# A mixture-of-experts layer and a GRU in one kernel: recurrent weights turned by VectorE in 32x32 squares, expert work one scan step later, three steps' rows sent from SBUF to SBUF

## The chip, the cores and the metric

One core of one Trainium2 chip. The metric is the device time of one execution of the program in microseconds (us), the median of several runs.

## What is computed

The input x is 8 sequences of 512 tokens with 256 features. A layer with one shared expert and 8 routed ones (two chosen per token) is added to x; then a GRU runs over the 512 tokens of each sequence, one after the other, and its output is added.

```python
# L0: x = x + (shared + routed) / 3
shared = silu(xf @ w1) * (xf @ w3) @ w2                 # 256 -> 512 -> 256
s = sigmoid(concat([xf, tf]) @ router_W)                # 8 scores, top 2 chosen
h = gelu(einsum('nc,ech->enh', xf, W1e)); y = einsum('enh,ehc->enc', h, W2e)
routed = einsum('ne,enc->nc', combine, y)
# L1: x = x + Ys, H has shape (8, 256)
Xz, Xr, Xh = X @ Wxz.T + bxz, X @ Wxr.T + bxr, X @ Wxh.T + bxh
for t in range(512):
    Z = sigmoid(Xz[t] + H @ Whz.T + bhz);  R = sigmoid(Xr[t] + H @ Whr.T + bhr)
    Ht = tanh(Xh[t] + (R * H) @ Whh.T + bhh)
    H = Z * H + (1 - Z) * Ht;  Y[t] = H @ Whq.T + bhq
```

## The kernel before, in words

**Tiles.** The tokens are cut into 32 tiles of 16 time steps: 8 sequences times 16 steps are 128 rows. Two tiles are a pair. For a pair the up products of the experts (`up`, L1111) run on both tiles at once, in three products of fp32r parts; the down products (`down`, through `product` L1083 in the scan and `full_product` L1119 ahead of it) run tile by tile. `accumulate` (L852) adds an expert's output to x on VectorE.

**Scan.** `body(n)` runs the 16 scan steps of tile n. A step is a ring of short operations on three engines: TensorE's product for gate r (L1247), ScalarE's tanh `t_r` (L693), VectorE's transposes `t_rT` (L982) and the product `rhT` (L985), TensorE's product for the candidate, ScalarE's `t_h` (L713), VectorE's transposes `terms` (L1006) and the scan instruction `hist` (L1009), which gives the next H. All else fills the gaps: each engine's program is written out by hand, and `place_of(n, s)` maps a scan step to a pair p and a place r of 32 in that pair's program; tables by r (`PROJ1`, `UP_ACT2`, `ADD2`, `TANH1`, `LATE_XT2`) say what is done there. `FIRST_STEP` sets the distance between s and r. Three things go by the step s itself and not by r: the ring, the seeds of the gate banks, and `keep_states` (L631), in which ScalarE copies the last tile's 16 states at s = 0.

```python
sp = s + TS * ((n + 1) % 2)
return (n + 1) // 2 + (sp >= FIRST_STEP), (sp - FIRST_STEP) % SPAN
```

**Gate inputs.** `project` multiplies a tile's x by the three input weights `wxT`; `add_bias` (L863) puts the result, half by half (q = 0, 1), into `xproj`. SP stores it to DRAM (`store_inputs`, L474), and `gate_rows` (L480) loads it again in the layout of the scan, `xs`: steps 0 to 7 first, steps 8 to 15 later. ScalarE's `seed_r` (L616) and `seed_zc` (L624) copy a step's row from `xs` to the gate banks. `load_late` (L464, L466) brings the x of later tiles in 17 transfers each: 16 of small squares, which VectorE transposes (`late_xT`, L899), and one of the plain tile.

**Head.** Ahead of the scan the first pair's experts run at full width. Here too the seven 256x256 GRU weights are loaded, 256 KB each (L415), and turned by TensorE in groups of four 128x128 transposes (L1058), emptied by ScalarE (L562) and VectorE (L748) in turn, the recurrent ones after GpSimd has put their columns in another order (L550). Then the first tile is transposed (`transpose_x1`, L1163) and projected, and some of the next tile's down products and the next pair's up products follow until the scan's first product. SP issues all transfers but three of the first ones; its queue, in order, is the weights, the initial state (L452), seven bias rows broadcast to 128 partitions (L455, L456), `load_late(4)`, the store and the rows of tile 0, and `load_late(5)`.

## Time and profile before

| | us |
|---|---|
| median of 3 runs | 1278.68 (1277.61 to 1278.76) |
| the profiled execution | 1277.44 |
| its span, first to last instruction | 1275.5 |
| TensorE busy | 1249.8 (98% of the span) |
| VectorE busy | 997.2 (78%) |
| ScalarE busy | 803.3 (63%) |
| GpSimd busy | 7.4 |

The granted TensorE clock was 1.0 of full speed throughout. The span runs from the first to the last instruction of the core; the time of an execution is 1.9 us longer. A busy TensorE is not one at its peak here, since the gaps of the scan are filled, at the end with products that nobody reads (`keep_busy`).

### The profile page before, as it was taken

What the parts mean: (1) busy time and instruction counts of PE and PEld (TensorE: products, weight loads), DVE (VectorE), ACT (ScalarE), POOL (GpSimd) and SP (SyncE); (2) the same over time, 40 slices, a digit from 0 to 9 for tenths busy, and PEclk for the clock granted to TensorE, in tenths of its full rate; (3) what the DMA queues carried; (4) which work ended last, traced back from release to release, by engine and by line L of the source; (5) the groups of instructions that cost most, each with busy time, mean ns of one, the idle gap of its engine ahead of it and who ended that gap; (6) DMA issues with size and microseconds to landing.
All of it is one profiled execution on the core that took longest, in us unless ns stands there. A gap on an engine that the chain in (4) does not pass through costs nothing.

```text
span 1275.5 us, 84499 instructions
## 1 busy us (share of the span) xinstructions
PE 1249.8 (98%) x35704; PEld 890.8 (70%) x35704; DVE 997.2 (78%) x6111; ACT 803.3 (63%) x4402; POOL 7.4 (1%) x25
## 2 busy tenths in 40 slices
PE   9999999999999999999999999999999999999887
PEld 8877677766677776667776667776667776666554
DVE  6678888788787888878888787887877787877765
ACT  4366666666666666666666666666666666666554
POOL 1000000000000000000000000000000000000000
PEclk9999999999999999999999999999999999999999
DMA  8211011111101111011111101111011111001110
GB/s 273 57 36 43 24 38 30 42 41 34 36 24 39 38 37 45 24 37 27 44 39 35 38 21 41 35 39 45 27 33 27 44 39 33 23 21 27 33 32 11
DMA packets 76186, 51.34 MB, mean 40 GB/s; under 512 B 40609, under 2 KB 73761, under 8 KB 75809
## 3 DMA queue, kind: packets, MB, share of 16 engines
q1 hardware_dynamic: 75128, 45.29, 13.7%
q8 instruction: 281, 4.60, 1.5%
q14 instruction: 97, 0.79, 0.2%
q10 hardware_dynamic: 680, 0.66, 0.2%
HBM read 29.13 MB, written 16.78 MB: 36 GB/s over the span
## 4 chain that ended last, share of the span: by engine, by line
PE 93%; DVE 3%; ACT 2%; issue 1%; DMA 1%; SPq 0%
PE dn_ps L1083 27%; PE up_ps L1111 26%; PE zc_bank L1247 21%; PE r_bank L1247 14%; PE aux L1083 2%; DVE terms L1006 2%; PE dn_ps L1119 1%; ACT t_h L713 1%; PE misc L1083 1%; DVE hist L1009 1%; DMA x_all<-in_L_cond_W1e 1%; DVE t_rT L982 1%; ACT t_r L693 0%; DVE rhT L985 0%; SPq L411 0%
## 5 line engine op out<-in xcount | busy, mean ns | idle before, releaser
L982 DVE STREAM_TRANSPOSE t_rT<-t_r 128x32 f32<-128x32 f32 x1024 | 156.2, 191 | 171.1 <-ACT t_r L693 163.6
L693 ACT ACTIVATE t_r<-r_bank 128x32 f32<-128x32 f32 x1024 | 146.1, 195 | 210.2 <-PE r_bank L1247 200.2
L713 ACT ACTIVATE t_h<-zc_bank 128x32 f32<-128x32 f32 x1024 | 145.9, 195 | 207.7 <-PE zc_bank L1247 207.7
L1083 PE MATMUL dn_ps<-we_sb,x_all 128*32 128x256 f32 (+1 forms) x5144 | 274.5, 329 | 0.0
L1247 PEld LDWEIGHTS zc_bank<-whT,rhT 128*8 128x8 f32 x8192 | 118.1, 87 | 177.5 <-DVE rhT L985 176.9
L1247 PE MATMUL r_bank<-whT,hist 128*8 128x64 f32 x8192 | 210.1, 220 | 16.0 <-DVE hist L1009 13.4
L1247 PE MATMUL zc_bank<-whT,rhT 128*8 128x64 f32 x8192 | 211.0, 220 | 2.8 <-DVE rhT L985 0.3
L1247 PE MATMUL zc_bank<-whT,hist 128*8 128x64 f32 x8192 | 208.9, 219 | 0.8 <-issue 0.8
L1006 DVE STREAM_TRANSPOSE terms<-t_h 128x32 f32<-128x32 f32 x1024 | 156.5, 192 | 38.2 <-ACT t_h L713 19.7
L1247 PEld LDWEIGHTS r_bank<-whT,hist 128*8 128x8 f32 x8192 | 117.6, 88 | 94.6 <-DVE hist L1009 72.5
L1083 PEld LDWEIGHTS dn_ps<-we_sb,x_all 128*32 128x32 f32 x5144 | 137.9, 110 | 31.9 <-issue 1.0
L1111 PE MATMUL up_ps<-x_high,we_high 128*128 128x256 f32 (+1 forms) x540 | 159.1, 295 | 0.2 <-DVE hid L820 0.2
L1111 PE MATMUL up_ps<-x_high,we_low 128*128 128x256 f32 (+1 forms) x540 | 155.4, 288 | 0.0
L1111 PE MATMUL up_ps<-x_low,we_high 128*128 128x256 f32 x526 | 154.9, 294 | 0.0
L624 ACT ACTIVATE zc_bank<-gru_raw 128x128 f32<-128x128 f32 x512 | 144.3, 282 | 16.0
L1009 DVE TENSOR_TENSOR_SCAN hist<-factors,terms 128x16 f32<-128x16 f32 x1024 | 145.4, 184 | 0.0
L1247 PEld LDWEIGHTS zc_bank<-whT,hist 128*8 128x8 f32 x8192 | 142.4, 90 | 0.2
L990 DVE STREAM_TRANSPOSE factors<-a_row 128x64 f32<-128x64 f32 x512 | 126.0, 246 | 19.5 <-ACT a_row L704 1.4
L985 DVE SCALAR_TENSOR_TENSOR rhT<-t_rT,hist 128x8 f32<-128x8 f32 x1024 | 133.3, 168 | 0.0
L704 ACT ACTIVATE a_row<-t_z 128x64 f32<-128x64 f32 x512 | 125.7, 245 | 0.0
L852 DVE SCALAR_TENSOR_TENSOR x_all<-dn_ps,gates_all,x_all 128x256 f32<-128x256 f32 x256 | 121.3, 474 | 5.6 <-PE dn_ps L1119 1.9
L616 ACT ACTIVATE r_bank<-gru_raw 128x64 f32<-128x64 f32 x512 | 114.3, 223 | 3.4 <-DMA gru_raw<-gate_inputs_by_group 3.4
(132 smaller groups left out, 1691.4 us busy)
## 6 DMA issues: line engine op xcount, KB each, us to landing
gate_inputs_by_group<-gru_raw SPq DMA_DIRECT2D x64, 192.0 KB, 2.0
gru_raw<-gate_inputs_by_group SPq DMA_DIRECT2D x256, 48.0 KB
xT_all<-in_x SPq DMA_DIRECT2D x448, 8.0 KB
x_all<-in_x SPq DMA_DIRECT2D x31, 128.0 KB
out<-gru_raw SPq DMA_DIRECT2D x31, 128.0 KB
x_all<-in_L_cond_W1e SPq DMA_DIRECT2D x4, 512.0 KB, 7.6
we_sb<-in_L_cond_W2e SPq DMA_DIRECT2D x4, 512.0 KB, 8.6
xT_all<-in_L_cond_w SPq DMA_DIRECT2D x2, 256.0 KB, 5.3
```

Source lines behind the costliest of these rows:

```text
L624: act.activation(zc_bank[:, 0:2 * GW], xs[:, s, GW:RW], ACT.Copy).then_inc(seeded_zc, 1)
L693: act.activation(t_r[:, i, :], r_ps[:, i * Q:(i + 1) * Q], ACT.Tanh, scale=0.5).then_inc(tr_ready, 1)
L704: act.activation(a_row[:, :, :], t_z[:, :, :], ACT.Copy, bias=0.5, scale=-0.5).then_inc(a_ready, 1)
L713: act.activation(t_h[:, i, :], c_ps[:, i * Q:(i + 1) * Q], ACT.Tanh, scale=-1.0).then_inc(th_ready, 1)
L982: dve.transpose(t_rT[:, i, :], t_r[:, i, :]).then_inc(trT_done, 1)
L985: dve.scalar_tensor_tensor(rhT[:, i, :], t_rT[:, i, 0:B], 1.0, old[:, i, :], ALU.add, ALU.mult)\
L990: dve.transpose(factors[:, :, :, 1].rearrange("p i q -> p (i q)"), a_row[:, :, :].rearrange("p i q -> p (i q)"))\
L1006: dve.transpose(terms[:, i, :, 0], t_h[:, i, :]).then_inc(thT_done, 1)
L1009: dve.tensor_tensor_scan(hist[:, s, i, :, :].rearrange("p b e -> p (b e)"), factors[:, i, 0:B, :].rearrange("p b e -> p (b e)"), terms[:, ...
L1083: done = pe.matmul(ps[Q * j:Q * (j + 1), col:col + cols], lhsT[:, Q * j:Q * (j + 1)], rhs, start=first, stop=last, tile_position=(0, Q * j ...
L1111: done = pe.matmul(up_ps[place % 2][:, half * PAIR + begin * P:half * PAIR + end * P], w, (x_low if low_x else x_high)[:, p % 2, begin:end ...
L1247: done = pe.matmul(ps[Q * j:Q * j + B, :], lhsT[:, k, :], whT[:, gate, k, j * GW:(j + 1) * GW], start=False, stop=(k == NI - 1), tile_posi ...
```

## The change

1. **Weights.** No GRU weight passes TensorE, ScalarE or GpSimd any more. Each is loaded in four transfers that bring it in a cut by which VectorE's transposes of 32x32 squares give the final layout (`load_wx`, `load_blocks`, `turn_wx`, `turn_wh`). The transfers are issued after all other weights and the biases: 12 of 64 KB in runs of 128 bytes for the input weights, 16 of 64 KB in runs of 256 bytes for the recurrent ones. The factor 0.5 on Whh is now an own operation of ScalarE.
2. **Places.** `FIRST_STEP` is 7 and no longer 6: everything placed by r comes one scan step later. The head loses the down products of place 9 and six up products (`FIRST_UPS` 30 and no longer 36), which the first scan step takes.
3. **Rows.** The rows of the first three steps of a tile go straight from `xproj` to `xs`, 12 more transfers per tile (`step_rows`); the way over DRAM stays for the others. `load_late(4)` moves behind the rows of tile 0.

```diff
-        raw = [gru_raw[:, r, :, :] for r in range(7)]
-        ordered = {r: gru_raw[:, 7 + i, :, :] for i, r in enumerate((1, 3, 5, 6))}
+        RB = C // Q
+        wx_blocks = [gru_raw[:, g, :, :].rearrange("p o c -> p (o c)").rearrange("p (k n q) -> p k n q", k=KC, q=Q) for g in range(GATES)]
+        BLOCK_HOME = 6
...
-        ROUND_TR = [[], [], [("w", 0), ("w", 1)], [("w", 2)], [("w", 3), ("w", 4)], [("w", 5), ("w", 6)], [], []]
...
-        FIRST_STEP = 6
+        FIRST_STEP = 7
...
-        UP_ACT2_FIRST = {12: 3, 15: 4, 18: 5, 20: 6, 23: 7, 25: 8, 27: 9, 29: 10, 31: 11}
+        UP_ACT2_FIRST = {9: 2, 12: 3, 15: 4, 18: 5, 20: 6, 23: 7, 25: 8, 27: 9, 29: 10, 31: 11}
...
-        FIRST_UPS = 36
+        FIRST_UPS = 30
...
@@ SP
+            def load_blocks(blocks, w, loaded):
+                by_row = w.rearrange("(n r) c -> r n c", r=Q)
+                for j in range(NG):
+                    sp.dma_start(blocks[Q * j:Q * (j + 1), :, :], by_row[:, :, GW * j:GW * (j + 1)]).then_inc(loaded, 16)
+            def load_wx(g):
+                by_row = gru_wx[g].rearrange("(n r) (k c) -> r k n c", r=Q, k=KC)
+                for j in range(NG):
+                    sp.dma_start(wx_blocks[g][Q * j:Q * (j + 1), :, :, :], by_row[:, :, :, Q * j:Q * (j + 1)]).then_inc(ld_wx[g], 16)
...
+            for g in range(GATES):
+                load_wx(g)
+            sp.wait_ge(shared_ready, 2)
+            for g in range(GATES + 1):
+                load_blocks(wh_blocks[g], gru_wh[g], ld_wh[g])
...
-            load_late(EARLY)
...
+            def step_rows(s, q):
+                for j in range(q * NG // PIECES, (q + 1) * NG // PIECES):
+                    sp.dma_start(xs[Q * j:Q * j + B, s, :], xproj[s::TS, j, :]).then_inc(xs_step[s], 16)
+            def deliver(t, q):
+                sp.wait_ge(xp_ready, PIECES * t + q + 1)
+                step_rows(0, q)
+                store_inputs(t, q)
+                for s in range(1, AHEAD):
+                    step_rows(s, q)
...
@@ ACT, end of the head and seeds
+            act.wait_ge(wh_turned, GATES * NI)
+            act.activation(whT[:, 2, :, :], whT[:, 2, :, :], ACT.Copy, scale=0.5).then_inc(whh_halved, 1)
             consume_up(1, 1)
-            act.wait_ge(xs_first, 16 * NG)
+            act.wait_ge(xs_step[0], 16 * NG)
...
@@ DVE
+            def turn_wx(g):
+                dve.wait_ge(ld_wx[g], 16 * NG)
+                for k in range(KC):
+                    dve.transpose(wxT[:, k, :, COLS[g]].rearrange("p j (b r) -> p j b r", r=Q),
+                                  wx_blocks[g][:, k, :, :].rearrange("p (j b) q -> p j b q", j=NG)).then_inc(wx_turned, 1)
...
                 accumulate(0, e - 1)
+                if e >= NE - 2:
+                    turn_wx(e - NE + 2)
...
             accumulate(0, NE - 1)
-            gate_biases()
+            turn_wx(2)
             accumulate(0, NE)
             accumulate(1, 0)
-            for q in range(PIECES):
-                add_bias(0, q)
+            gate_biases()
+            add_bias(0, 0)
+            turn_wh(0)
+            add_bias(0, 1)
+            turn_wh(1)
+            turn_wh(2)
             shared_silu(1, 0)
             shared_hidden(1, 0)
+            turn_wh(3)
```

Below is how the change moves instructions. First VectorE at the end of the head, from the accumulation of the sixth down product on (`x_all<-dn_ps,gates_all,x_all` is `accumulate`, `we_low` a split of an expert's weights, `bias_rows` the sum of two biases, `gru_raw<-dn_ps,bias_rows` is `add_bias`). Before:

```order
L939 COPY hist<-h0T 128x8 x2
L852 SCALAR_TENSOR_TENSOR x_all<-dn_ps,gates_all,x_all 128x256
L827 TENSOR_TENSOR x_low<-xT_all,x_high 128x512
L852 SCALAR_TENSOR_TENSOR x_all<-dn_ps,gates_all,x_all 128x256 x2
L808 TENSOR_TENSOR bias_rows<-xT_all 128x4x64 x3
L852 SCALAR_TENSOR_TENSOR x_all<-dn_ps,gates_all,x_all 128x256
L852 SCALAR_TENSOR_TENSOR x_all<-dn_ps,x_all 128x256
L863 TENSOR_TENSOR gru_raw<-dn_ps,bias_rows 128x384 x2
```

Now:

```order
L858 SCALAR_TENSOR_TENSOR x_all<-dn_ps,gates_all,x_all 128x256
L752 STREAM_TRANSPOSE wxT<-gru_raw 128x4x64 x2
L833 TENSOR_TENSOR x_low<-xT_all,x_high 128x512
L858 SCALAR_TENSOR_TENSOR x_all<-dn_ps,gates_all,x_all 128x256
L752 STREAM_TRANSPOSE wxT<-gru_raw 128x4x64 x2
L858 SCALAR_TENSOR_TENSOR x_all<-dn_ps,gates_all,x_all 128x256
L752 STREAM_TRANSPOSE wxT<-gru_raw 128x4x64 x2
L858 SCALAR_TENSOR_TENSOR x_all<-dn_ps,gates_all,x_all 128x256
```

The transposes of the input weights now stand between the last accumulations. After `add_bias(0, 0)` follow those of the recurrent weights:

```order
L869 TENSOR_TENSOR gru_raw<-dn_ps,bias_rows 128x384
L760 STREAM_TRANSPOSE whT<-x_all 128x256 x2
L869 TENSOR_TENSOR gru_raw<-dn_ps,bias_rows 128x384
L760 STREAM_TRANSPOSE whT<-x_all 128x256 x4
L820 SCALAR_TENSOR_TENSOR gru_raw<-gru_raw,up_ps 128x256
L826 TENSOR_TENSOR hid<-gru_raw,up_ps 128x256
L760 STREAM_TRANSPOSE wqT<-x_all 128x256 x2
```

Eight transposes stand ahead of and between the operations that the head's last down and up products wait for.

Second, ScalarE in the scan, the last step of a tile with even n and the first of the next (`score` is the tanh of the router, placed at r = 25; `gru_raw<-hist` is `keep_states`). Before:

```order
L704 ACTIVATE a_row<-t_z 128x64
L573 ACTIVATE score<-logits 128x16
L713 ACTIVATE t_h<-zc_bank 128x32 x2
L624 ACTIVATE zc_bank<-gru_raw 128x128
L693 ACTIVATE t_r<-r_bank 128x32 x2
L695 ACTIVATE t_z<-zc_bank 128x64
L616 ACTIVATE r_bank<-gru_raw 128x64
L704 ACTIVATE a_row<-t_z 128x64
L631 ACTIVATE gru_raw<-hist 128x256
L713 ACTIVATE t_h<-zc_bank 128x32 x2
```

Now:

```order
L702 ACTIVATE a_row<-t_z 128x64
L627 ACTIVATE gru_raw<-hist 128x256
L569 ACTIVATE score<-logits 128x16
L711 ACTIVATE t_h<-zc_bank 128x32 x2
L620 ACTIVATE zc_bank<-gru_raw 128x128
```

The router's tanh has come into the step of `keep_states`, between it and `t_h`.

Third, SP's queue from the last bias row to the rows of tile 0, now (before, the 17 transfers of `load_late(4)` stood here, then two stores and eight loads):

```order
L447 DMA bias_q<-in_L_cond_bhq 128x256
L412 DMA gru_raw<-in_L_cond_Wxr 32x16x32 x4
L412 DMA gru_raw<-in_L_cond_Wxz 32x16x32 x4
L412 DMA gru_raw<-in_L_cond_Wxh 32x16x32 x4
L406 DMA x_all<-in_L_cond_Whr 32x8x64 x4
L406 DMA x_all<-in_L_cond_Whz 32x8x64 x4
L406 DMA x_all<-in_L_cond_Whh 32x8x64 x4
L406 DMA x_all<-in_L_cond_Whq 32x8x64 x4
L479 DMA gru_raw<-gru_raw 8x192 x2
L468 DMA gate_inputs_by_group<-gru_raw 128x2x192
```

All 28 weight transfers are issued between the biases and the first row of tile 0.

## Rows read from the trace of the kernel before

**Rows 1.** The page: span.

```profile
span 1275.5 us, 84499 instructions
```

**Rows 2.** Timeline of VectorE (start us, duration us): first and last scan instructions.

```profile
52.94 0.28 DVE L1009 TENSOR_TENSOR_SCAN hist<-factors,terms 128x16 f32<-128x16 f32 x2
...
1270.53 0.28 DVE L1009 TENSOR_TENSOR_SCAN hist<-factors,terms 128x16 f32<-128x16 f32 x2
```

**Rows 3.** Timeline of TensorE in the head, up to the projection.

```profile
22.77 0.60 PE L1058 MATMUL zc_bank<-ident,gru_raw 128*128 128x128 f32 x4
23.20 1.03 PE L1119 MATMUL dn_ps<-we_sb,x_all 128*128 128x256 f32 x4
...
26.31 1.03 PE L1119 MATMUL dn_ps<-we_sb,x_all 128*128 128x256 f32 x4
...
40.66 0.38 PE L1163 MATMUL misc<-ident,x_all 128*128 128x128 f32 x2
...
41.59 2.77 PE L1119 MATMUL dn_ps<-wxT,x1T 128*128 128x384 f32 x8
```

**Rows 4.** Timeline of VectorE in the head.

```profile
24.48 0.68 DVE L748 TENSOR_SCALAR wxT<-zc_bank 128x512 f32<-128x512 f32 x1
...
25.68 0.48 DVE L852 SCALAR_TENSOR_TENSOR x_all<-dn_ps,gates_all,x_all 128x256 f32<-128x256 f32 x1
```

**Rows 5.** The DMA issues: how many, KB each, median us from issue to landing.

```profile
gate_inputs_by_group<-gru_raw SPq DMA_DIRECT2D x64, 192.0 KB, 2.0
xT_all<-in_L_cond_bxr SPq DMA_DIRECT2D x1, 128.0 KB, 4.6
bias_q<-in_L_cond_bhq SPq DMA_DIRECT2D x1, 128.0 KB, 7.1
```

**Rows 6.** Timeline of SP's queue: start and length of the issues.

```profile
25.88 0.36 SPq L455 DMA_DIRECT2D xT_all<-in_L_cond_bxr  x1
...
29.70 0.43 SPq L456 DMA_DIRECT2D bias_q<-in_L_cond_bhq  x1
30.17 8.29 SPq L464 DMA_DIRECT2D xT_all<-in_x  x16
...
51.54 10.30 SPq L464 DMA_DIRECT2D xT_all<-in_x  x16
```

**Rows 7.** Window 18:24 (last: DMA share, GB/s); DMA packets of 36:36.5 and 36:37.

```profile
18.00:24.00 6.00, 6.00 (x42) 5.64 (x41) 5.32 (x24) 3.49 (x7) 0.00 (x0) 1.00 1.10 348
DMA packets 453, 0.09 MB, mean 184 GB/s; under 512 B 403, under 2 KB 453, under 8 KB 453
DMA packets 766, 0.12 MB, mean 124 GB/s; under 512 B 716, under 2 KB 766, under 8 KB 766
```

**Rows 8.** Groups of VectorE by shape: a 32x32 transpose of 128x256.

```profile
L899 DVE STREAM_TRANSPOSE xT_all<-xT_all 128x256 f32<-128x256 f32 x28 | 11.8, 423 | 0.0
```

**Rows 9.** Timeline of VectorE and TensorE between projection and scan.

```profile
44.40 0.56 DVE L863 TENSOR_TENSOR gru_raw<-dn_ps,bias_rows 128x384 f32<-128x384 f32 x1 [0.73 <-PE dn_ps L1119]
47.77 0.48 DVE L852 SCALAR_TENSOR_TENSOR x_all<-dn_ps,gates_all,x_all 128x256 f32<-128x256 f32 x1
46.69 2.79 PE L1119 MATMUL dn_ps<-we_sb,x_all 128*128 128x256 f32 x16
49.12 0.47 PE L1111 MATMUL up_ps<-x_high,w_high 128*128 128x256 f32 x1
50.81 0.41 PE L1247 MATMUL r_bank<-whT,hist 128*8 128x64 f32 x16
```

**Rows 10.** Timeline of ScalarE, last step of a tile and first of the next.

```profile
469.28 0.20 ACT L573 ACTIVATE score<-logits 128x16 f32<-128x16 f32 x1
469.77 0.29 ACT L713 ACTIVATE t_h<-zc_bank 128x32 f32<-128x32 f32 x2 [0.29 <-PE zc_bank L1247]
...
471.62 0.62 ACT L631 ACTIVATE gru_raw<-hist 128x256 f32<-128x256 f32 x1
472.17 0.28 ACT L713 ACTIVATE t_h<-zc_bank 128x32 f32<-128x32 f32 x2
```

More of the change, by code:

```diff
@@ L151, in moe_then_gru @@
         ld_h0 = sem("ld_h0")
-        ld_gru_x = sem("ld_gru_x")
-        ld_gru_h = sem("ld_gru_h")
+        ld_wx = [sem(f"ld_wx{g}") for g in range(GATES)]
+        ld_wh = [sem(f"ld_wh{g}") for g in range(GATES + 1)]
+        wx_turned = sem("wx_turned")
+        wh_turned = sem("wh_turned")
+        whh_halved = sem("whh_halved")
         ld_bias = sem("ld_bias")
@@ L190, in moe_then_gru @@
         xs_second = sem("xs_second")
+        xs_step = [sem(f"xs_step{s}") for s in range(AHEAD)]
         bits_set = sem("bits_set")
@@ L438, in _ @@
             load_we1(1)
-            for r, part, _ in WEIGHTS:
-                if part == "x":
-                    load_gru(r, ld_gru_x)
             load_we1(2)
             load_we2(1)
-            for r, part, _ in WEIGHTS:
-                if part != "x":
-                    load_gru(r, ld_gru_h)
             load_we1(3)
@@ L562, in take @@
                 act.activation(dst, src, ACT.Copy, scale=s).then_inc(tr_act, 1)
-            def take_round(e):
-                for m in in_round(e):
-                    if m % 2 == 0:
-                        take(m)
             def score_tanh(i, tiles):
@@ L696, in body @@
                     if after:
-                        if s + 1 == HALF:
+                        if after[1] < AHEAD:
+                            act.wait_ge(xs_step[after[1]], 16 * NG * (after[0] + 1))
+                        if after[1] == AHEAD:
+                            act.wait_ge(xs_first, 16 * NG * (n + 1))
+                        if after[1] == HALF:
                             act.wait_ge(xs_second, 16 * NG * (n + 1))
-                        if last:
-                            act.wait_ge(xs_first, 16 * NG * (n + 2))
                         seed_r(*after)
@@ L748, in take, with turn_wh @@
                 dve.tensor_scalar(dst, src, s, None, ALU.mult).then_inc(tr_dve, 1)
-            def take_round(e):
-                for m in in_round(e):
-                    if m % 2 == 1:
-                        take(m)
+            def turn_wx(g):
[3 more added lines that the diff above has]
+                                  wx_blocks[g][:, k, :, :].rearrange("p (j b) q -> p j b q", j=NG)).then_inc(wx_turned, 1)
+            def turn_wh(g):
+                dve.wait_ge(ld_wh[g], 16 * NG)
+                for i in range(NI):
+                    dst = whT[:, g, i, :] if g < GATES else wqT[:, i, :]
+                    dve.transpose(dst.rearrange("p (n r) -> p n r", r=Q), wh_blocks[g][:, :, Q * i:Q * (i + 1)]).then_inc(wh_turned, 1)
             def add_base(i, tiles):
```

95 lines of the change are left out of this document (31 added, 64 removed).

## The prediction, made blind

> **What bounds the kernel now.** I read four views in this order: the span, the timeline of VectorE over the whole scan, the timelines of the head, and the timeline of ScalarE inside a step. The span is 1275.5 us [rows 1]. The first scan instruction starts at 52.94, the last at 1270.53 [rows 2]: 511 steps in 1217.6 us, 2.383 us each. The same length holds at the end, where TensorE only runs products that nobody reads. So it is the ring of one step over three engines, and not TensorE's work, that sets the scan; TensorE's 98% is filling. The time is then the head up to the scan's first product at 50.81 [rows 9], 512 rings, and the last tile's output. Two things can move it: where the head ends, and what gets into the ring. That `FIRST_STEP` moves products into or out of the scan is worth nothing in itself, since the gaps hold them.
>
> In the head TensorE has no gap from 17 us on: its transposes, down products and up products stand back to back [rows 3].
>
> **The change, part by part** (all times on the clock of before).
>
> *Transposes off TensorE.* A group of four costs TensorE 0.43 us, from 22.77 to the next product's start at 23.20 [rows 3]. Seven groups are 3.0 us. Three of them stand ahead of the down product at 26.31 [rows 3]; without them it could start 1.3 sooner, at 25.0, but it waits for the accumulation of 25.68. VectorE is full there; it loses only the emptying at 24.48 (0.60 us to the next start), so the accumulation ends at about 25.6 and the product starts at 25.65, 0.65 sooner [rows 3, 4]. The other four groups give 1.7 in full. Shift: 2.35 us.
>
> *Where the input weights arrive.* Seven loads of 256 KB leave the front of the queue: 1.8 MB at 348 GB/s [rows 7] is 5.3 us. The last bias row lands at 29.70 + 7.1 = 36.8 now [rows 5, 6], so 31.5 then. Twelve 64 KB pieces of 512 packets of 128 bytes follow. No row has such a piece, so it is bounded. From 36.0 to 36.5 the engines took 403 small packets beside 50 of 1 KB [rows 7]; at 348 GB/s a 1 KB packet holds one of 16 engines for 47 ns, so the small ones took (8 - 2.35)/403 = 14 ns each, 0.45 us per piece. From 36 to 37 they took 716 in 1 us: 0.72 us per piece. The last of Wxh lands at 36.9 or at 40.1. I take 36.9, since the first half microsecond is the one with a queue behind it. VectorE then needs two transposes (0.423 each, 0.37 from start to start as I estimate: 0.75) [rows 8] and the last accumulation (0.48), which stands behind them; the tile's transpose on TensorE, now at 40.66 [rows 3], could start at 38.2. TensorE itself arrives at 40.66 - 2.35 = 38.3. The two meet; I lose 0.2 to their closeness and keep a shift of 2.1. Behind a late weight stand the accumulations, and TensorE's down products behind those: each us after 37.0 is a us of the head.
>
> *From the projection to the scan.* TensorE's work ahead of the scan loses three of twelve half products (2.43 us for all twelve, from 46.69 to 49.12: 0.6) and six of twelve up products (1.69 us for all from 49.12 to 50.81: 0.8) [rows 9], 1.4 us. Not all of it comes through. The ninth half product waits for `accumulate(1, 1)`, at 47.77 now and in time. VectorE gets six more transposes ahead of it behind the second `add_bias` of 44.40 (three pairs, 2.2 us), and the idle time there absorbs 0.6: it ends at 49.4 in place of 48.25 [rows 9]. The half product (0.2) and six up products (0.8) follow: scan at 50.4. Gain 0.4; without the stall it would be 1.4. The first pair of recurrent transposes fits into the gap between the two `add_bias`.
>
> *Rows of steps 0 to 2.* The head's way over DRAM takes two landings; the direct one takes one, of about 2.0 [rows 5]. ScalarE's seed then waits for nothing: TensorE's path is the later one. This is worth 0 beyond what the point above counts. In the scan each tile's SP queue gets 12 more issues of some 0.33 us each, 4 us of 38; the row of step 0 is ready about 3 us ahead of its seed. 0.
>
> *SP's queue.* Biases end at 24.5 there (6.8 us sooner than 30.2, less some blocking); 28 weight issues at 0.52 each (8.29/16) [rows 6] end at 39 if the queue takes them, and at 41 to 42 if it blocks behind 31.5. Tile 0's rows need it at 41.3. Between, 0 to 1 late, hidden by the slack of the seed.
>
> *load_late(4).* It moves from 30.17, where nobody waited, behind the rows of tile 0: it takes the place of `load_late(5)`, whose 16 issues start at 51.54 and last 10.3 [rows 6]; with the last transfer and its landing 14 us. Issued at about 48.9 it lands at 63.0. VectorE turns it at the end of step 5, at 62.5. VectorE has 0.7 us idle before the next `t_rT`, the transpose takes 0.42: loss 0.2, at worst 1.7, at best 0.
>
> *ScalarE in the ring.* This is what I count against the change. At s = 0 `keep_states` starts at 471.62 and `t_h` follows at 472.17 with no idle time between; one step before, `t_h` came after 0.29 idle, beside the router's tanh at 469.28 [rows 10]. So `keep_states` just fits and the tanh fits in its own step. With places one step later the tanh (r = 25) comes into the step of `keep_states`, ahead of `t_h`. It takes 0.20, and the next instruction can start about 0.12 after it (the seeds and `t_z` follow each other at 0.12 to 0.15). `t_h` is in the ring, so each such step gets 0.12 longer: 14 pairs (p = 1 to 14), **1.7 us** in all. Bounds: 0.05 each (0.7) if the engine overlaps more, 0.20 each (2.8) if it doesn't at all. GpSimd's copies and the halving of Whh lie beside other work: 0.
>
> **Sum.** -2.1 - 0.4 + 0.2 + 1.7 = -0.6 us. The profiled execution of 1277.44 becomes 1276.8. The median of the runs shown is 1.24 above that execution; I forecast on the median: **1278.1 us**. About 0.2% (2.6 us) is what a measurement of this kernel can tell from no change, so this is no change that can be told.
>
> **Rivals.**
> 1. *Small packets hold up the head (slower).* With 0.72 us per piece Wxh lands at 40.1, the tile's transpose starts at 41.4, 0.8 later than now, and the scan 0.4 later. All of SP's queue is 3 us later, so `load_late(4)` costs about 1 us. 0.4 + 1.0 + 1.7 = +3.1: 1281.8. For it: from 36 to 37 the engines weren't full and still gave no more. Against: the queue had run dry in that microsecond. It decides from a landing at about 39.5.
> 2. *A piece costs as much as a bias row (slower).* Seven bias rows of 128 KB land from 30.5 to 36.8, 1.05 us apart, where 348 GB/s would give 0.37 [rows 5 to 7]. At 1.05 for each of 12 pieces Wxh lands at 44.1 and the scan starts 4.4 late; with 1.0 and 1.7, +7.1: 1285.8. Against: these rows all read one KB 128 times over, the weights do not.
> 3. *The head gains all, the ring loses little (faster).* 2.35 + 0.9 (half of the stall gone, since transposes of VectorE overlap) with 0.7 in the ring: -2.6 or more, 1276.1 to 1275.3. For it: TensorE's share of the head is certain.
> 4. *The tanh hides after all*, so that only the head counts: -2.3, 1276.4, in between.
>
> The Trainium skill speaks against the change here: "DMA: Bandwidth & Descriptors", section Bandwidth, calls transfers under 64 KB descriptor-dominated and gives 0.95 us of DMA time for one of 64 KB (issued from GpSimd). By that, as an estimate, twelve pieces take 11.4 us and the time is near rival 2. The rows of packets above give half of it, and I follow them.
>
> **How the numbers follow.** Forecast and rival 4 (1276.2 to 1280) 0.61; rival 1 0.15, rival 2 0.05, rival 3 0.19. Range: from rival 3 without its last us, 1275.5, to rival 1, 1281.9. Faster by over 0.2% needs under 1276.1: rival 3, 0.20. Slower needs over 1281.2: rival 2 and most of rival 1, 0.17. Between: 0.63.
>
> **What would show it.** Scan's first product at about 48.3 (head right); at 46.5 or less, rival 3; after 50, rivals 1 and 2, with VectorE idle ahead of the `wxT` transposes for a DMA. In the scan: `t_h` at s = 0 of odd n about 0.12 later than its neighbours and 14 steps of 2.50 among those of 2.38; if they have 2.38, the ring term is wrong. An idle time of VectorE ahead of `late_xT` in step 5 shows the late load. If steps in general are longer than 2.383, something has entered the ring that I haven't seen, and the prediction is wrong altogether.

## The result, and the profile after

The changed kernel takes **1286.09 us** (median of 7 runs, 1282.42 to 1288.06), the kernel before in the same series 1278.68 (7 runs, 1277.52 to 1280.02). The ratio is 1.0051, interval 1.0039 to 1.0063: slower by 0.5%. I had said 1278.1, with a range of 1275.5 to 1281.9, and no change. The profiled execution of after took 1284.21 us, that of before 1277.44.

The page of after and its timeline of VectorE (start us, duration us), the lines that answer to [rows 1, 2]:

```profile
span 1282.4 us, 84924 instructions
53.85 0.28 DVE L1019 TENSOR_TENSOR_SCAN hist<-factors,terms 128x16 f32<-128x16 f32 x2
...
1277.47 0.28 DVE L1019 TENSOR_TENSOR_SCAN hist<-factors,terms 128x16 f32<-128x16 f32 x2
```

The first scan instruction starts 0.91 us later than before, the last 6.94 us later. Taking the scan instructions of the timeline one after the other, the end of tile 0 stands at 91.8 us (89.2 before), so the rest of tile 0 lost 1.7 and tiles 1 to 31 lost 4.3. Three places, then: head, tile 0, ring.

**Head.** The weights came as forecast. Timeline of VectorE, then of TensorE, to be held against [rows 3, 9]:

```profile
37.29 0.77 DVE L752 STREAM_TRANSPOSE wxT<-gru_raw 128x256 f32<-128x256 f32 x2 [1.05 <-DMA gru_raw<-in_L_cond_Wxh]
...
41.00 0.56 DVE L869 TENSOR_TENSOR gru_raw<-dn_ps,bias_rows 128x384 f32<-128x384 f32 x1 [1.22 <-PE dn_ps L1121]
...
42.29 0.56 DVE L869 TENSOR_TENSOR gru_raw<-dn_ps,bias_rows 128x384 f32<-128x384 f32 x1
...
46.29 0.77 DVE L760 STREAM_TRANSPOSE wqT<-x_all 128x256 f32<-128x256 f32 x2 [1.35 <-DMA x_all<-in_L_cond_Whq]
```

```profile
44.65 1.91 PE L1121 MATMUL dn_ps<-we_sb,x_all 128*128 128x256 f32 x10
48.27 0.49 PE L1121 MATMUL dn_ps<-we_sb,x_all 128*128 128x128 f32 x2 [1.72 <-DVE x_all L858]
...
50.56 0.61 PE L1253 MATMUL r_bank<-whT,hist 128*8 128x64 f32 x16 [1.09 <-ACT r_bank L612]
```

The second `add_bias` stands at 42.29, 2.11 us ahead of the 44.40 of [rows 9]. But the scan's first product stands at 50.56, only 0.25 ahead. TensorE is idle twice on the way: 1.72 us for an accumulation that VectorE could start only after `Whq` had landed, and 1.09 for ScalarE's seed. The queue of SP shows why (start, length, number of issues), and ScalarE's timeline what it did:

```profile
32.82 2.65 SPq L412 DMA_DIRECT2D gru_raw<-in_L_cond_Wxh  x4
35.52 2.10 SPq L406 DMA_DIRECT2D x_all<-in_L_cond_Whr  x4
...
41.60 1.93 SPq L406 DMA_DIRECT2D x_all<-in_L_cond_Whq  x4
43.66 1.34 SPq L479 DMA_DIRECT2D gru_raw<-gru_raw  x2
45.04 0.44 SPq L468 DMA_DIRECT2D gate_inputs_by_group<-gru_raw  x1
45.52 3.62 SPq L479 DMA_DIRECT2D gru_raw<-gru_raw  x6
...
52.12 3.23 SPq L474 DMA_DIRECT2D gru_raw<-gate_inputs_by_group  x8
55.41 1.72 SPq L460 DMA_DIRECT2D xT_all<-in_x  x1
```

```profile
44.74 0.37 ACT L576 ACTIVATE gru_raw<-up_ps 128x256 f32<-128x256 f32 x1
50.28 0.23 ACT L612 ACTIVATE r_bank<-gru_raw 128x64 f32<-128x64 f32 x1 [5.17 <-DMA gru_raw<-gru_raw]
```

SP gets through the weights at 43.6 us, and the last two rows of step 0 are issued as the fifth and sixth transfer of its next block, behind a store and four rows of steps 1 and 2, at 47.97. They land 5.17 us after ScalarE had nothing else to do. A transfer of one row from SBUF to SBUF takes SP 0.60 us to issue (3.62 for six); one of rows from DRAM 0.40 here (3.23 for eight).

Then something that I hadn't in my sum at all. The windows of TensorE's granted clock (busy time and count of each engine; behind them the clock, the DMA share and GB/s):

```profile
46.00:48.00 2.00, 0.56 (x3) 0.16 (x1) 1.68 (x5) 0.00 (x0) 0.00 (x0) 1.00 0.32 106
48.00:50.00 2.00, 1.20 (x8) 0.99 (x8) 0.70 (x2) 0.00 (x0) 0.00 (x0) 1.00 0.04 10
50.00:52.00 2.00, 1.44 (x44) 1.41 (x48) 0.51 (x4) 0.93 (x5) 0.00 (x0) 0.54 0.31 105
52.00:54.00 2.00, 2.00 (x33) 1.29 (x23) 0.81 (x6) 0.97 (x5) 0.00 (x0) 0.60 0.15 48
54.00:56.00 2.00, 2.00 (x69) 1.43 (x68) 1.44 (x9) 1.20 (x7) 0.00 (x0) 1.00 0.42 99
```

From 46 to 50 TensorE had 1.76 of 4 us busy; from 50 to 54 it got 0.54 and 0.60 of its clock, near the 1.2 GHz level of its two (1.2 and 2.4). The first step is the longer for it: its r product took 0.61 us (0.41 in [rows 9]), and from the first product to the first scan instruction it is 3.29 us (2.13 before). The 0.25 gained became 0.91 lost. It is the clock and not the work that the new places put into this step: in e14 below, with the same places and a clock of 1.0, the stretch is 2.12.

**Tile 0.** Timeline of VectorE:

```profile
66.00 0.28 DVE L1019 TENSOR_TENSOR_SCAN hist<-factors,terms 128x16 f32<-128x16 f32 x2
68.26 0.45 DVE L905 STREAM_TRANSPOSE xT_all<-xT_all 128x256 f32<-128x256 f32 x1 [1.97 <-DMA x_all<-in_x]
```

`load_late(4)`, issued from 55.41, lands at 68.2: VectorE waits 1.97 us, and one scan step takes 4.0 us in place of 2.4, 1.6 longer.

**Ring.** Most steps still take 2.38 us. The exceptions are regular (medians over the tiles 2 to 28): step 0 of the odd tiles 2.51, their steps 1 and 2 both 2.41, step 0 of the even tiles 2.41. ScalarE and VectorE in step 0 of tile 5, to be held against [rows 10]:

```profile
245.96 0.63 ACT L627 ACTIVATE gru_raw<-hist 128x256 f32<-128x256 f32 x1
246.50 0.20 ACT L569 ACTIVATE score<-logits 128x16 f32<-128x16 f32 x1
246.61 0.26 ACT L711 ACTIVATE t_h<-zc_bank 128x32 f32<-128x32 f32 x2
```

```profile
246.81 0.31 DVE L1016 STREAM_TRANSPOSE terms<-t_h 128x32 f32<-128x32 f32 x2 [0.27 <-ACT t_h L711]
```

The tanh stands between `keep_states` and `t_h`, as forecast. Steps 1 and 2 have none, and are longer all the same.

### The profile page after: what moved, and what is told of

Its sections match the earlier page's. It is cut to its first block, busy times and chain, and to the rows that moved or that the text cites. A ratio compares the mean times of both kernels' runs of the same rounds, so it can differ in the third digit from the quotient of the medians.

```text
span 1282.4 us, 84924 instructions
## 1 busy us (share of the span) xinstructions
PE 1251.2 (98%) x35684; PEld 889.7 (69%) x35684; DVE 997.1 (78%) x6121; ACT 805.9 (63%) x4400; POOL 3.9 (0%) x17
## 4 chain that ended last, share of the span: by engine, by line
PE 86%; SPq 5%; DVE 4%; ACT 3%; issue 1%; DMA 0%
PE dn_ps L1085 26%; PE up_ps L1113 23%; PE zc_bank L1253 20%; PE r_bank L1253 14%; PE aux L1085 2%; DVE terms L1016 2%; ACT t_h L711 1%; DVE hist L1019 1%; SPq L412 1%; PE misc L1085 1%; ACT t_r L689 1%; SPq L460 1%; ACT gru_raw L627 1%; SPq L406 1%; SPq L479 1%
```

## The experiments

Each run gives its median, the number of its executions, and its ratio to the kernel before on the same chip (1279.4 to 1280.0 us in every series). Times inside an execution are from its one profile; two profiles of one kernel can differ by 1.7 us in the head (e15), so smaller differences there show little. Unless said otherwise, an edit is made to the changed kernel.

### Each cause alone

**e1.** The rows of step 0 of both halves go first on SP's queue.

```diff
-for q in range(PIECES): deliver(0, q)
+for q in range(PIECES):
+    sp.wait_ge(xp_ready, q + 1)
+    step_rows(0, q)
+for q in range(PIECES):
+    store_inputs(0, q)
+    for s in range(1, AHEAD): step_rows(s, q)
```

> Of tile 0 the rows of step 0 are issued for both halves before the store and the rows of steps 1 and 2. In the changed kernel SP issued the second half's step-0 rows at 47.97 and 48.58, behind four others of 0.6 us each; they landed at 50.26 and TensorE stood idle from 49.5 to 50.56, then ran the first step at half clock. Theory A (queue order and load_late(4) are coupled): the scan's first product comes at about 49.4 in place of 50.56, step 0 loses its extra 1.0 us, so the first scan instruction starts 2.0 us sooner, about 51.9. But SP reaches load_late(4) no sooner, so step 5 ends in a wait that is longer by the same 2 us (4 in place of 2), and the time stays within 0.5 us of the changed kernel (+7.4 on before). Theory B (the two losses are separate): 2 us less than the changed kernel.

Measured: 1286.61 (5 runs), 1.0059 [1.0046, 1.0072]. The seed of step 0 came at 48.02, 2.3 earlier, but the next one waited 2.93 us for the rows of step 1, the clock fell, and the first scan instructions ended at 54.0 as in the change. One row had been put ahead of another on a full queue. Theory A's total came out (no gain), but not its way: the first scan instruction is no sooner.

**e2, e3.** `load_late(4)` issued by GpSimd at the program's start with a semaphore of its own (e2), and both edits (e3).

> load_late(4), 17 transfers, goes to GpSimd's queue at the start of the program, where GpSimd has nothing to do; SP issues load_late(5) in its place. Theory A: VectorE's wait of 1.97 us ahead of the turning of tile 4's x (step 5, at 66.3) goes, and with it 1.6 us of the time: +5.8 on before. The head stays as it is (first product at 50.5). Theory B (the wait was slack): no gain, since the next wait takes it over. If the load disturbs the head's saturated DMA traffic, the wxT transposes wait longer and the first product is up to 1 us later.

> Both edits of the two runs before. Theory A (coupled): here both gains come, 2.0 from the start and 1.6 to 2.0 from the missing wait: about 3.8 us less than the changed kernel, +3.6 on before. Theory B (separate): the sum of what the two gave alone.

Measured: 1287.82 (6 runs), 1.0062 [1.0050, 1.0074], and 1285.78 (5 runs), 1.0050 [1.0038, 1.0062]. In both the late wait is gone (that step takes 2.40), but the first step ends 2.9 and 1.6 us later than in the change. The last bias row is issued at 26.42 and 25.91 (23.44 in the change), Wxr is turned at 34.38 and 35.03 (32.46; 31.56 to 33.48 in all other profiles with the squares), Wxh at 39.42 and 39.18 (37.29; 36.24 to 38.41). What tile 0 gained, the head gave back.

**e4.** The tanh behind `seed_zc` in ScalarE's order.

```diff
-if EARLY <= 2 * p + 2 < NT and r == TANH1: score_tanh(...)
 ...
 if after: seed_zc(*after)
+if EARLY <= 2 * p + 2 < NT and r == TANH1: score_tanh(...)
```

> The router's tanh is issued at the end of its step, behind t_h and the seed, in place of between keep_states and t_h. Theory A: steps s = 0 of odd n fall from 2.51 to 2.41 us (not to 2.38, since the added wait on ScalarE remains), 14 times 0.10 = 1.4 us less than the changed kernel, +6.0 on before. Theory B (the step is long because of keep_states alone, the tanh is hidden): no change.

Measured: 1285.44 (5 runs), 1.0046 [1.0034, 1.0058]. Step 0 of the odd tiles went from 2.51 to 2.40; steps 1 and 2 stayed at 2.41. The tanh is 0.10 us, 14 times: theory A.

**e5.** As e4, and ScalarE's waits for the rows of steps 1, 2 and 3 to 7 at the end of the step before.

> The change with two edits to ScalarE's scan loop: its wait for the rows of steps 1, 2 and 3 to 7 stands at the end of the step before, and the score's tanh of the odd tiles stands behind the seed of z and c. Theory A (the added waits of ScalarE in steps 0, 1 and 2 cost the ring 0.03 us each): steps 0, 1 and 2 of every tile return from 2.40 to 2.42 us to 2.38, which is about 3.3 us of the 6.0 that the scan lost, and the median goes from 1286.1 to about 1282.5. Theory B (these steps are longer because the router's products and VectorE's work moved into them): steps 1 and 2 of the odd tiles stay at 2.41 and only step 0 of the odd tiles gets shorter (2.50 to 2.40, 1.5 us), as in the run with the tanh alone; the median stays above 1284.

Measured: 1290.14 (6 runs), 1.0082 [1.0067, 1.0097], worse by 4.7 than e4. Steps 0, 1 and 2 of *all* tiles take 2.43 to 2.44. Both theories failed, but the result points at the waits: the same three, 0.02 to 0.06 dearer ahead of `t_r` than ahead of the seed.

**e6.** The kernel before with only the table of places.

```diff
-FIRST_STEP = 6
+FIRST_STEP = 7
-UP_ACT2_FIRST = {12: 3, 15: 4, ...
+UP_ACT2_FIRST = {9: 2, 12: 3, 15: 4, ...
-FIRST_UPS = 36
+FIRST_UPS = 30
-consume_up(1, 2)
```

> The kernel before with only the table of places changed (all expert work one scan step later, six ups fewer ahead of the scan); weights and rows as before. Theory A (the places cost only the tanh behind keep_states): step 0 of the 14 odd tiles goes from 2.38 to about 2.49 us, steps 1 and 2 stay at 2.38, the first scan instructions end about 0.4 us earlier or at the same time, and the median is 1279.5 to 1280.5. Theory B (the places are also what makes steps 1 and 2 longer): these go to 2.41 as in the change, another 0.06 us for each odd tile, and the median is 1281 to 1282.

Measured: **1293.70** (6 runs), 1.0104 [1.0082, 1.0126], far beyond both theories. Steps 1 and 2 are 2.38, so the places don't lengthen them; step 0 of the odd tiles, where the tanh now stands, is 2.46. ScalarE's waits, and one of them:

```profile
ACT r_bank L616 <- DMA gru_raw<-gate_inputs_by_group: 17.2, 18, 3.5
435.58 0.23 ACT L616 ACTIVATE r_bank<-gru_raw 128x64 f32<-128x64 f32 x1 [1.78 <-DMA gru_raw<-gate_inputs_by_group]
```

Expert work one step later also means the projection, and so the rows, one step later. In before the seed at the end of a tile never waits; here it does 17 times, 13.7 us in all (17.2 less the 3.5 of the head). The direct rows take this away: in the change ScalarE waits for rows only once, in the head.

**e7, e8.** ScalarE issues the four rows of step 0 of tile 0 (e7); besides, `turn_wh(3)` behind the accumulates and `load_late(4)` by GpSimd behind its memset (e8).

> The change with one edit: ScalarE issues the four transfers that bring tile 0's rows of step 0 (two behind x1's copy, two behind the first sigmoid), so that they no longer stand behind the 16 issues of Wh on SyncE's queue. Theory A (SyncE's queue sets the head): the rows land at about 46.3 us instead of 50.3, and ScalarE's seed of r follows; the first product of the scan then waits for accumulate(1,1) behind Whq and stands at about 49.3 instead of 50.6, the clock does not fall or falls for less, and the first scan instructions end at 51.5 to 52.5 instead of 54.1; the rows of steps 1 and 2 and the late loads come 2.4 us earlier as well, so step 6's wait of 1.6 us falls away or stays under 1. Median 1282.5 to 1284. Theory B (the tensor engine's idle time before the scan is set by Whq alone): the first scan instructions end above 53 and the median is 1285 or more.

> The change with three edits outside the ring: step 0's rows issued by ScalarE as in the run above, turn_wh(3) behind the two accumulates of the second pair, and tile 4's 17 late loads issued by GpSimd behind its memset of the rows. Theory A (head and late wait are three separate losses that add up): the first scan instructions end at 50.5 to 51.5 us, step 6 of tile 0 takes 2.40, no granted clock under 0.9 in the first scan steps, and the median is 1280.5 to 1282.5, the ring's 3.3 us being left. Theory B (one loss uncovers the next): the rows of steps 1 and 2 on SyncE's queue or GpSimd's transfers, which share the 16 DMA engines with Whq, come too late in their turn, one of the steps 1 and 2 takes over 3 us, and the median stays above 1283.

Measured: 1284.75 (6 runs), 1.0049 [1.0033, 1.0064], and 1285.92 (5 runs), 1.0043 [1.0031, 1.0055]. In e7 the first step ended at 53.0, 1.1 sooner, but the second took 3.3 us (clock 0.52 and 0.63 from 50 to 54, behind 2.06 us of idle time) and the one with the late load 3.5; that is nearer to theory B. In e8 the late wait was gone and the first seed stood at 47.3, but the next waited 3.6 us for the rows of step 1, and the first step ended at 54.7: theory B of e8, with the long wait inside step 0.

**e9.** `AHEAD = 1`: rows of steps 1 to 7 over DRAM, one added wait instead of three.

> The change with AHEAD 1 instead of 3: only the rows of step 0 go from SBUF to SBUF, those of steps 1 to 7 through DRAM; so of the three added waits of ScalarE (in steps 0, 1 and 2) one is left, in step 0. Theory A (each added wait costs the ring its 0.03 us, wherever it stands): steps 1 and 2 of all tiles go back to 2.38 us, step 0 stays at 2.40 and 2.50, which is 14 x 0.06 = 0.9 us less; with 8 issues of 0.6 us fewer on SyncE's queue in the head, the late loads come about 3 us earlier (they start once the second store has landed), and step 6's stall of 1.6 us falls away: median 1282.5 to 1284.5. Theory B (steps 1 and 2 are longer because of the work that the places put there): they stay at 2.41. Rival on the head: the rows of step 1 now wait for a store and a load through DRAM, land at about 53 us, and step 1 of tile 0 takes up to 3.5 us, which gives back 1 us.

Measured: 1289.34 (6 runs), 1.0064 [1.0046, 1.0081]. Steps 1 and 2 went to 2.38, as theory A says; but step 0 now waits for rows over DRAM in about a third of the tiles (up to 0.7 us each). Whether the sum is worse than the change's can't be told: the change had 1.0051 [1.0039, 1.0063] and, in e15, 1.0066 [1.0051, 1.0081]. It is not better, as theory A had hoped.

**e10.** The change with the places of before.

> The change with the places as before (expert work from scan step 6, 36 ups ahead of the scan), weights and rows as in the change. Theory A (places and waits collide: the longer steps 0, 1 and 2 need both the added wait and the work moved beside it): step 0 of the odd tiles goes to 2.40 or less without the tanh, steps 1 and 2 to 2.38 or 2.40; the median is 1281.5 to 1284, still above before, because the head and the late loads are as in the change, and one up more stands ahead of the scan. Theory B (the places cost nothing once the rows come early, all of the loss is in rows and head): the median stays within 1 us of the change's 1286.

Measured: 1292.12 (5 runs), 1.0087 [1.0074, 1.0100]. The ring is at 2.41 in steps 0, 1 and 2 of the odd tiles, so the waits lengthen steps 1 and 2 without the places. Neither theory had the time, though. Most of it is in tile 0: `load_late(4)` is now needed a step earlier.

```profile
DVE xT_all L906 <- DMA x_all<-in_x: 5.7, 1, 5.7
66.00:68.00 2.00, 0.00 (x0) 0.00 (x0) 0.00 (x0) 0.00 (x0) 0.00 (x0) 1.00 0.09 12
68.00:70.00 2.00, 0.00 (x0) 0.00 (x0) 0.32 (x1) 0.00 (x0) 0.00 (x0) 0.58 0.34 81
70.00:72.00 2.00, 1.53 (x20) 1.32 (x21) 1.46 (x12) 0.82 (x4) 0.00 (x0) 0.50 0.12 17
```

That is 5.7 us of waiting, and half the clock behind it; tile 0 ends at 97.8 (91.8 in the change).

**e11, e12.** Only the weights' change: places and rows as before, but `load_late(4)` still behind the rows of tile 0 (e11); besides, tile 0's step-0 rows by ScalarE and `turn_wh(3)` behind the accumulates (e12).

> The kernel before with its recurrent weights loaded in squares and turned by VectorE, as in the change; places, and rows through DRAM, as before. Theory A (the squares bring the projection forward by 2.1 us, but SyncE's queue holds 16 more issues until 43.6 us, so nothing of it reaches the rows): stores issued at 43.6 and 44.1 instead of 43.7 and 44.9, the rows of steps 0 to 7 land at about 51 us, the first scan instructions end at 53.5 to 55, every later step is 2.38 us except for step 5 or 6, which waits up to 2 us for tile 4's late loads; median 1279.5 to 1282. Theory B (the weights are a gain by themselves): the median is under 1278.

> The same with two edits more: tile 0's rows of step 0 go from SBUF to SBUF, issued by ScalarE (four transfers), and turn_wh(3) stands behind the two accumulates; all other rows go through DRAM as before, so the ring has no added wait but one in tile 0's step 0. Theory A (the head's gain is real once the first rows pass around SyncE's queue): the first product of the scan at about 48.3 us instead of 50.8, the rows of steps 1 to 7 land at 50.5 to 51.5 and step 1 is 0.5 to 1.5 us longer, the first steps end 1 to 2 us earlier than before, the rest at 2.38 us per step but for a wait of up to 2 us for the late loads: median 1277.5 to 1280. Theory B (each transfer that is advanced delays another): step 1 or step 5 takes over 4 us, and the median is over 1280.

Measured: 1281.03 (12 runs), 1.0012 [1.0001, 1.0023], and 1279.87 (11 runs), 0.9998 [0.9987, 1.0009]. The squares with the later `load_late(4)` cost 1 us, at the edge of what can be told; ScalarE waits 6.0 us for its first rows in e11. The late load cost nothing in either, though it is needed as early as in e10: without the twelve direct rows of tile 0, at 0.6 us each, SP's queue gets to it at 49.15 and 49.68 (57.48 in e10). Both medians lie in the range of their theory A.

### The waits, and the sum

**e13.** From tile 1 on TensorE instead of ScalarE waits for these rows, ahead of the r product.

> The change with one edit: from tile 1 on TensorE, not ScalarE, waits for the rows of steps 1, 2 and 3 to 7, ahead of the r product of the step before, where it stands idle for the state anyway; ScalarE's seed of r is covered by its wait for the z product, as in step 15 it still waits itself. Theory A (the 0.03 us are the additional wait in ScalarE's own queue, which lies in the ring): steps 1 and 2 of the odd tiles return to 2.38 us, step 0 of the even tiles keeps at most the wait that it had, and step 0 of the odd tiles stays at 2.47 to 2.50 because of the tanh; 1 to 3 us less than the change, median 1283 to 1285. Theory B (a wait costs the ring the same wherever it stands): the periods stay at 2.40 to 2.50 and the median within 1 us of the change's.

Measured: **1301.24** (5 runs), 1.0190 [1.0168, 1.0213]. The scan instruction and the r product behind it, on VectorE and on TensorE, first in a step without the wait, then in one with it:

```profile
245.14 0.28 DVE L1019 TENSOR_TENSOR_SCAN hist<-factors,terms 128x16 f32<-128x16 f32 x2
...
247.52 0.28 DVE L1019 TENSOR_TENSOR_SCAN hist<-factors,terms 128x16 f32<-128x16 f32 x2
```

```profile
245.40 0.40 PE L1253 MATMUL r_bank<-whT,hist 128*8 128x64 f32 x16
...
247.86 0.41 PE L1253 MATMUL r_bank<-whT,hist 128*8 128x64 f32 x16
```

The r product starts 0.34 instead of 0.26 behind the scan instruction, and the three steps take 2.46 to 2.50 (2.55 with the tanh). Theory A had taken the wait to be free where the engine stands idle for the state; it cost 0.08. Theory B failed too, since the run is 13 us above the change.

The 0.08 doesn't explain all of this. In the profile tiles 1 to 31 take 21 us more than before; the medians of steps 0, 1 and 2 account for some 10. The rest is in single steps, longer by 0.2 to 1.3 us (31 of them, 6 in the change), and TensorE's weight loads for the r product stand idle 67 times, 15.6 us in all, with nothing that the profile shows to wait for. What that is stays open.

**e16.** The counterproof: the kernel before with three waits whose value is long reached, and nothing else.

```diff
 if last: act.wait_ge(xs_first, 16 * NG * (n + 2))
+if 1 <= s + 1 <= 3: act.wait_ge(xs_first, 16 * NG * (n + 1))
 seed_r(*after)
```

> The kernel before with three waits more in ScalarE's scan loop, ahead of the seeds of steps 1, 2 and 3, on a value of the rows' semaphore that was long reached; nothing else. It measures the added wait by itself. Theory A (a wait that has nothing to wait for still costs the ring 0.03 us in steps in which VectorE is full): steps 0, 1 and 2 of the odd tiles go from 2.38 to 2.41 us and step 0 of the even ones to 2.40, as in the run with the places undone, some 2 us in all: median 1280.5 to 1282 where before has 1279.5. Theory B (it is the transfers of the rows beside the steps, or the semaphores' updates, and not the wait): all periods stay at 2.38 and the median within 0.5 us of before.

Measured: **1281.42** (9 runs), 1.0022 [1.0012, 1.0032], 2.0 us above before. Steps 0, 1, 2 of the odd tiles take 2.41, step 0 of the even ones 2.41, their step 3 2.39, the rest 2.38: the pattern of the change, without its transfers: theory A. VectorE in step 1 of tile 5, first of before, then of e16:

```profile
245.14 0.31 DVE L982 STREAM_TRANSPOSE t_rT<-t_r 128x32 f32<-128x32 f32 x2 [0.67 <-ACT t_r L693]
245.39 0.26 DVE L985 SCALAR_TENSOR_TENSOR rhT<-t_rT,hist 128x8 f32<-128x8 f32 x2
245.68 0.25 DVE L990 STREAM_TRANSPOSE factors<-a_row 128x64 f32<-128x64 f32 x1
...
246.56 0.29 DVE L1009 TENSOR_TENSOR_SCAN hist<-factors,terms 128x16 f32<-128x16 f32 x2
```

```profile
245.43 0.30 DVE L984 STREAM_TRANSPOSE t_rT<-t_r 128x32 f32<-128x32 f32 x2 [0.67 <-ACT t_r L693]
245.68 0.26 DVE L987 SCALAR_TENSOR_TENSOR rhT<-t_rT,hist 128x8 f32<-128x8 f32 x2
246.01 0.25 DVE L992 STREAM_TRANSPOSE factors<-a_row 128x64 f32<-128x64 f32 x1
...
246.88 0.28 DVE L1011 TENSOR_TENSOR_SCAN hist<-factors,terms 128x16 f32<-128x16 f32 x2
```

From `rhT` to `factors` it is 0.33 instead of 0.29, since ScalarE's `a_row`, which stands behind the seed, starts 0.32 instead of 0.27 after `t_z`. Behind `factors` stand two of the router's operations and then `terms` and the scan, back to back; so the 0.04 arrives at the scan as 0.03. In steps 1 and 2 of the even tiles the same wait costs nothing (2.38), and the steps 7 and 15, in which before has its waits, are no longer than others.

**e14.** Places, rows and weights as in the change, with TensorE's waits, the tanh moved, `turn_wh(3)` late, `load_late(4)` on GpSimd, step 0's rows by ScalarE, those of steps 1 and 2 ahead of the stores.

> The change with the causes found so far removed together: the waits on TensorE as in the run above, the score's tanh of the odd tiles behind the seed of z and c, tile 0's rows of step 0 issued by ScalarE, those of steps 1 and 2 ahead of the two stores on SyncE's queue, turn_wh(3) behind the accumulates, tile 4's late loads on GpSimd behind its memset. Theory A (ring, head and late loads are the whole loss, and they are separate): the steps of tile 0 from the second on take 2.38 to 2.6 us, those of the other tiles 2.38 but for 2.40 to 2.41 in step 0, and the first step's scan instructions end at 51 to 53 us; the median is 1277.5 to 1280.5, as before within the measurement. Theory B (what is mended in the head is given back): a wait of over 1 us in tile 0 stays, and the median is over 1281.

Measured: 1299.39 (5 runs), 1.0167 [1.0148, 1.0186]. The ring lost to TensorE's waits as in e13. The head is right: first scan instruction at 49.39, 4.5 us sooner than in the change. But the third step waits 2.9 us for the rows that go over the stores, as theory B has it:

```profile
49.39 0.28 DVE L1042 TENSOR_TENSOR_SCAN hist<-factors,terms 128x16 f32<-128x16 f32 x2
52.11 0.28 DVE L1042 TENSOR_TENSOR_SCAN hist<-factors,terms 128x16 f32<-128x16 f32 x2
57.42 0.28 DVE L1042 TENSOR_TENSOR_SCAN hist<-factors,terms 128x16 f32<-128x16 f32 x2
ACT r_bank L623 <- DMA gru_raw<-gate_inputs_by_group: 2.9, 1, 2.9
```

**e15.** The change again, on that chip.

> The change itself once more, beside the two runs above on the same chip, because its executions lay 5.6 us apart and those of the kernel before 2.5. If the losses are three fixed ones, the median is 1285 to 1287 again; if the wait for the late loads depends on when DMA descriptors land, the profile's step 6 of tile 0 differs from 4.0 us by more than 0.5, and the spread of the executions is again over 4 us.

Measured: 1287.77 (6 runs, 1283.76 to 1289.00), 1.0066 [1.0051, 1.0081]. Its profile has the first step's end at 55.9 (54.1 in the first profile): ScalarE waited 6.3 for the first rows there, `wqT` 1.3 for Whq, and VectorE waited only 1.2 for the late load (a step longer by 0.9). So the losses of the head are fixed in kind, not in size.

**e17.** As e14, but the waits on ScalarE as in the change, and the two stores ahead of the rows of steps 1 and 2.

> The change with the head of the run e14, one order changed, and the tanh, but with its own waits on ScalarE: step 0's rows issued by ScalarE, then on SyncE's queue first the two stores, then the rows of steps 1 and 2, turn_wh(3) behind the accumulates, tile 4's late loads on GpSimd. Theory A (head, late loads, tanh and waits add up): tile 0's last scan instruction at 86.5 to 88.5 us (91.8 in the change, 89.2 before), steps 0 of the odd tiles 2.40, steps 1 and 2 of them 2.41, and a median of 1280 to 1282.5, of which 2 us are the waits. Theory B (what the head gains comes back as a wait in tile 1 or later): tile 0's end is early but the median stays over 1283.

Measured: **1279.51** (11 runs), 1.0007 [0.9996, 1.0017]. No difference to before can be told, and the change itself had 1286 and 1288; it is a little below the 1280 to 1282.5 of theory A. SP's queue, and the scan:

```profile
43.55 1.89 SPq L469 DMA_DIRECT2D gate_inputs_by_group<-gru_raw  x2
45.48 4.95 SPq L480 DMA_DIRECT2D gru_raw<-gru_raw  x8
50.48 3.73 SPq L475 DMA_DIRECT2D gru_raw<-gate_inputs_by_group  x8
```

```profile
50.65 0.28 DVE L1041 TENSOR_TENSOR_SCAN hist<-factors,terms 128x16 f32<-128x16 f32 x2
53.32 0.28 DVE L1041 TENSOR_TENSOR_SCAN hist<-factors,terms 128x16 f32<-128x16 f32 x2
55.95 0.29 DVE L1041 TENSOR_TENSOR_SCAN hist<-factors,terms 128x16 f32<-128x16 f32 x2
```

Tile 0 ends at 87.3 (91.8 in the change, 89.2 before). Head, late load and tanh add up. What tile 0 gains on before (1.9) is what the added waits then cost (2.0 in e16).

**e18.** The version to which the runs point: squares and the head of e17, but places and the loop's rows as in before, so that the ring has no added wait from tile 1 on.

> The version to which the runs point: squares turned by VectorE and the head of the run above, but places and the rows of all tiles but the first as in the kernel before (through DRAM, no added wait from tile 1 on). Theory A: the first step's scan instructions end at 49.5 to 51 us (53.2 before), step 2 or 3 waits up to 1 us for the rows of steps 3 to 7, all other steps as before; tile 0's end at 86.5 to 88.5, median 1276.5 to 1278.5, which is 1 to 3 us under before. Theory B (the earlier scan only waits longer in tile 0 or 1): median within 0.5 us of before or above.

Measured: **1277.85** (11 runs), 0.9992 [0.9983, 1.0001]. All regular steps are 2.38, tile 0 ends at 88.5. Its first step ends at 52.4, later than I expected and 1.5 us behind e17. Its first product stands at 49.98 (47.30 in e17), 2.7 later: its places put 1.4 us more of down and up products ahead of the scan, TensorE is idle 0.91 for an accumulation (VectorE had waited 0.80 for Whh), and 0.3 were lost earlier. e17 gives 1.2 of this back, since its first step is 3.35 us long, with 1.38 of waiting for the rows of step 1 (2.13 in e18). The interval reaches 1, so e18 may equal before; it is the lowest median of all.

## Why the prediction was wrong, point by point

- **What bounds the kernel** (ring and head): right. All of the loss lies there. But I wrote that what moves outside the ring "is worth nothing in itself". The order of the work also sets when the projection is ready, and e6 shows 14 us for that alone. In the change the direct rows pay this back, so the blind sum came out right at that point for a reason that I hadn't seen.
- **Transposes off TensorE, landing of Wx**: right. Wxh was forecast for 36.9 and turned at 37.29; the shift of 2.1 was 2.11. The last bias row was issued at 23.44 and took 7.8 us, to 31.2, so twelve pieces took 6.1 us, 0.51 each; I had taken 0.45. The Trainium skill's 0.95 us ("DMA: Bandwidth & Descriptors", Bandwidth) is for a single 64 KB transfer issued from GpSimd; as the price of each of these twelve it isn't borne out here. Rivals 1 and 2 are out by the landing (36.9 forecast, 40.1 and 44.1 theirs). Two things look like them and aren't: the sign "after 50" came (50.56, with VectorE idle 1.05 for Wxh), and the time is rival 2's 1285.8 almost exactly. Both are chance; neither comes from the pieces.
- **From projection to scan**: wrong. First product forecast 48.3, measured 50.56. I had the second accumulation end at 49.4 less the shift of 2.1, so 47.3, held up by six transposes; it ended 0.9 later, held up by the landing of Whq, the last weight on SP's queue. Another 1.1 is the wait for ScalarE's seed.
- **"SP's queue: 0 to 1 late, hidden by the slack of the seed", "Rows of steps 0 to 2: 0"**: this is the step that failed in the head. The queue was free at 43.6, not 41 to 42, and then the first step's last rows were the eighth transfer of their kind behind it, with a store among them, at 0.60 us each and not at 0.33. I took the price of an issue from rows out of DRAM, though no row of before had one between two places in SBUF, and gave it no bounds. ScalarE's seed then waited 5.17 us. In e17 the first seed waits 0.94 and stands at 45.75, and the first step ends 3.2 sooner.
- **The clock** was no term at all. Behind 2.8 us of idle time in two pieces the first step took 1.2 us more.
- **`load_late(4)`**: right mechanism, wrong size. Forecast 0.2 (at worst 1.7), measured 1.6 and 0.9 us of a longer step in the two profiles of the change; it was issued at 55.4, not at 48.9, again by SP's queue.
- **The tanh**: right. 14 steps of 2.51 among 2.41, 0.10 each (0.12 forecast), taken away by e4.
- **The added waits**: missing. The diff adds a wait to ScalarE in steps 0, 1 and 2, beside those that it had in 7 and 15. I read them as free since their rows land early. e16 prices them at 2.0 us by themselves. Beside SP's queue this is the other step that failed. The prediction had named the sign, that "something has entered the ring that I haven't seen"; it came in 4 of every 32 steps and not in general.
- **Sum against the runs**: tanh 1.4, waits 2.0, late load 1.6, head 0.9: 5.9 of the 6.9 by which the last scan instruction is late. The last 1.0 lies in single steps that are 0.1 to 1 us longer, which before has too; what causes those stays open, as does why the runs of the change spread over 5.6 us and those of before over 2.5.

## What to carry to other kernels

Ask of every wait that a change adds which engine executes it and how far the ring's next instruction is behind it, even where the value is long reached; here each cost 0 to 0.08 us, by place. A queue is a resource with a length: write out its issues between the last known free point and each consumer, with a duration for each *kind* of transfer, and when two things are late on it, reordering only chooses which. When a change has two halves (later work, earlier rows), price each alone: here one costs 14 us and the other takes that away.

## What the runs showed of the hardware that I hadn't expected

- A wait whose value is long reached lengthened the ring of 2.38 us by 0.03 us ahead of ScalarE's seed (e16), by up to 0.06 at the end of its step (e5), and by 0.08 ahead of TensorE's product (e13); in steps with slack behind it, by nothing (e16, steps 1 and 2 of the even tiles).
- An issue of 8 short rows from SBUF to SBUF took SP 0.60 us in the change (0.60 to 0.67 in the heads of e1, e9, e14 and e17), one of 64 KB in squares 0.48 to 0.53 for the recurrent weights and 0.66 to 1.44 for the input weights just behind the biases, one of rows from DRAM 0.32 to 0.47 where nothing was waited for in between (1.28 for four in before, 3.73 for eight in e17). GpSimd issued the late loads at 0.51 each; when they began behind its memset, the first product still stood at 47.3 in e14 and e17, but from the program's start on they came with a first step that ended 1.6 to 2.9 later, of which the spread between profiles may be a part.
- TensorE's granted clock was near 0.5 in the four microseconds behind two idle times of 1.72 and 1.09 us, and again in e10 behind 5.7 us. In e7 one idle time of 2.06 us was enough for 0.52 and 0.63. It isn't so each time: behind 3.41 us in e8, and behind 0.96 and 1.53 in e5, the clock stayed at 1.0. So idle times of a microsecond or two in the head can have a price beyond their own length; what decides it these runs don't show.
